# First attention: when GpSimd issues the eight row transfers of each head pair

## The reference, cut to what matters

```
scores = jnp.einsum('bhqd,bhkd->bhqk', qh, k_rec) / math.sqrt(d)
decay = jnp.exp(-LAMBDA_DECAY * jnp.abs(t[:, None] - t[None, :]))
scores = scores * decay[None, None, :, :]
attn = jax.nn.softmax(scores, axis=-1)
out = jnp.einsum('bhqk,bhkd->bhqd', attn, v_rec)
```

## Time and profile before

| what | us |
|---|---|
| median of 3 runs | 3543.53 |
| lowest, highest | 3539.63, 3559.12 |
| the profiled execution's own time | 3536.14 |
| its span, first to last instruction | 3534.2 |
| PE busy in the span | 2898.2 |
| DVE busy | 2095.9 |
| ACT busy | 1689.6 |
| POOL busy | 1095.5 |

### The profile page before, as it was taken

The page is one execution under the profiler, slowest core; times in us unless marked ns, Lnnn a source line. Parts: engine busy times, 40 slices in busy tenths (PEclk is TensorE's granted clock), DMA queues, the critical chain, the costliest instruction groups (busy, mean ns, idle before and its releaser), DMA issues. The chain is left out here.

```text
span 3534.2 us, 59852 instructions
## 1 busy us (share of the span) xinstructions
PE 2898.2 (82%) x18120; PEld 1813.4 (51%) x18120; DVE 2095.9 (59%) x4691; ACT 1689.6 (48%) x3357; POOL 1095.5 (31%) x1891
## 2 busy tenths in 40 slices
PE   6599999999983599977953999958688888797869
PEld 3234443444441589964522889824355555544434
DVE  6577777777628544445566444346477777436852
ACT  4256766677731354431122544413366667354535
POOL 3344443444401254431011544324322222020112
PEclk9679999999996799988976999979899999898879
DMA  7612222222213244330031444322211111000001
GB/s 260 228 61 74 78 73 71 76 75 76 68 60 120 73 88 90 80 76 12 0 120 54 81 93 91 58 63 83 79 50 52 50 52 51 20 1 13 0 14 48
DMA packets 171006, 248.63 MB, mean 70 GB/s; under 512 B 29752, under 2 KB 114104, under 8 KB 170832
## 3 DMA queue, kind: packets, MB, share of 16 engines
q1 hardware_dynamic: 138064, 211.81, 18.0%
q0 software_dynamic: 32768, 34.64, 6.1%
HBM read 152.94 MB, written 92.27 MB: 69 GB/s over the span
## 5 line engine op out<-in xcount | busy, mean ns | idle before, releaser
L1916 DVE CUSTOM_DVE_ANT_0 s0Ah_SD<-s0Ah_ps_s,s0Ah_table 128x1024 f32<-128x1024 f32 x512 | 607.2, 1222 | 210.7 <-PE s0Ah_ps_s L1971 164.1
L1940 ACT ACTIVATE s0Ah_PM<-s0Ah_ps_x 128x512 f32<-128x512 f32 x1024 | 533.7, 600 | 233.3 <-PE s0Ah_ps_x L1996 127.7
L1971 PE MATMUL s0Ah_ps_s<-s0Ah_plus_k,s0Ah_plus_q 48*128 48x512 f32 x1024 | 424.5, 479 | 67.4 <-DVE s0Ah_mx L1916 35.3
L1896 POOL TENSOR_TENSOR s0Ah_DG<-s0Ah_SD,s0Ah_mx 128x128 f32<-128x128 f32 x512 | 203.3, 404 | 469.4 <-DVE s0Ah_mx L1916 469.1
L1971 PEld LDWEIGHTS s0Ah_ps_s<-s0Ah_plus_k,s0Ah_plus_q 48*128 48x128 f32 x1024 | 168.1, 194 | 319.0 <-DVE s0Ah_mx L1916 214.4
L2182 ACT ACTIVATE s4Ch_PM<-s4Ch_SD,s4Ch_nb 128x260 f32<-128x260 f32 (+2 forms) x512 | 254.2, 497 | 146.0 <-POOL s4Ch_nb L2125 133.2
L2016 PE MATMUL s0Ah_ps_v<-s0Ah_PM,s0A_V 128*17 128x512 f32 x2048 | 273.6, 607 | 0.0
L2136 DVE CUSTOM_DVE_ANT_0 s4Ch_SD<-s4Ch_ps_s,s4Ch_table 128x260 f32<-128x260 f32 (+2 forms) x512 | 204.8, 407 | 77.7 <-PE s4Ch_ps_s L2227 62.1
L1996 PE MATMUL s0Ah_ps_x<-s0Ah_plus_q,s0Ah_plus_k 50*128 50x512 f32 (+3 forms) x640 | 238.3, 389 | 4.6 <-DMA s0Ah_minus_k<-s0A_parts 4.3
L2227 PE MATMUL s4Ch_ps_s<-s4Ch_ks,s4Ch_qs 96*128 96x256 bf16 (+2 forms) x896 | 141.5, 228 | 114.6 <-DVE s4Ch_mx L2136 58.8
L1996 PE MATMUL s0Ah_ps_x<-s0Ah_minus_q,s0Ah_minus_k 50*128 50x512 f32 (+3 forms) x640 | 219.0, 390 | 0.0
(11 more groups left out here) (420 smaller groups left out, 7314.4 us busy)
## 6 DMA issues: line engine op xcount, KB each, us to landing
s0A_parts<-s0Ap_sp_top SPq DMA_DIRECT2D x32, 512.0 KB, 5.4
s0A_parts<-s0Ap_sp_rest SPq DMA_DIRECT2D x32, 512.0 KB, 5.4
s1M_raw_w<-in_L_ffn_w SPq DMA_DIRECT2D x16, 1024.0 KB
s3M_raw_w<-in_L_ffn_w SPq DMA_DIRECT2D x16, 1024.0 KB
s4C_parts<-s4Cp_sp SPq DMA_DIRECT2D x48, 256.0 KB, 2.4
s0Ah_plus_q<-s0A_parts SPq DMA_DIRECT2D x64, 128.0 KB
s0Ah_plus_k<-s0A_parts SPq DMA_DIRECT2D x64, 128.0 KB
s0Ah_minus_q<-s0A_parts SPq DMA_DIRECT2D x64, 128.0 KB
```

The costliest lines, as they stand in the source:

```text
L1896: nc.gpsimd.tensor_tensor(DG[p % 3][:, r * TB + t, :], SD[i % NSD][:, t * P:(t + 1) * P], mx[p % 3][:, r * TB + t:r * TB + t + 1].to_broad ...
L1916: nc.vector.tensor_tensor_reduce(SD[i % NSD][:, :], ps_s[i % 2][:, :, :].rearrange("p a n -> p (a n)"), table[:, (TB - 1 - t) * P:(TB - 1 ...
L1940: nc.scalar.activation(PM[n % NPB][:, :], ps_x[u % NX][:, :], ACT.Exp).then_inc(e_ok, 1)
L1971: x = nc.tensor.matmul(ps_s[i % 2][:, half, :], q[at(r), t * P:(t + 1) * P], k[at(r), half * GT:(half + 1) * GT], start=True, stop=True)
```

## The change

POOL's eight transfers are no longer issued in one piece after the fourth block of the next pair. `rest_of` still stands there, but the transfers follow two at a time, behind the fifth, sixth, seventh and eighth block. For the last pair, which has no blocks behind it, all eight still follow `rest_of` directly. `maxima` takes the head and the part as arguments. The number of transfers, their order and their sizes stay as they were.

```
-            def maxima(p):
+            def maxima(p, r, n):
                 pool.wait_ge(nr_ok, START + p + 1)
-                for r in range(2):
-                    for n in range(2):
-                        for q in (plus[p % 4][0], minus[p % 2][0]):
-                            z = r * 64 + SROW + n
-                            pool.dma_start(q[z:z + 1, :].bitcast(F32).rearrange("a (t q) -> a t q", t=TB),
-                                         NMp[p % 2][n][r * TB:(r + 1) * TB, :].bitcast(F32)).then_inc(rows_in[p % 2], 16)
+                for q in (plus[p % 4][0], minus[p % 2][0]):
+                    z = r * 64 + SROW + n
+                    pool.dma_start(q[z:z + 1, :].bitcast(F32).rearrange("a (t q) -> a t q", t=TB),
+                                   NMp[p % 2][n][r * TB:(r + 1) * TB, :].bitcast(F32)).then_inc(rows_in[p % 2], 16)
...
                                         ALU.subtract).then_inc(nr_ok, 1)
-                maxima(p)
...
                 if i % U == 3 and p:
                     rest_of(p - 1)
+                if 4 <= i % U < 8 and p:
+                    maxima(p - 1, i % U // 2 - 2, i % 2)
             rest_of(NP - 1)
+            for r in range(2):
+                for n in range(2):
+                    maxima(NP - 1, r, n)
```

## The result

| | before | after |
|---|---|---|
| median us (6 runs each) | 3544.64 | 3606.68 |
| lowest, highest | 3539.49, 3566.25 | 3600.34, 3623.05 |
| span of the profiled execution | 3534.2 | 3603.4 |

The ratio is 1.0168, 95% interval 1.0136 to 1.0201. The change makes the kernel 1.7% slower, 62 us by the medians and 69 by the two profiled spans. I had forecast 17 us less, so the sign was wrong.

The account below looks back on a forecast made before the run. PE's work and the round of loads were taken as nearly equal bounds. 10.8 us from 27 pairs plus 6.0 from pair 15 made 16.8 us less, 3543.5 to 3526.7, so 3527 us; range 3512 to 3544.

Parts of the forecast that it names:

- What bounds the kernel: In the changed stage, PE's work (24.53 us a pair) and the round of loads (24.97) were said to bind almost equally.
- POOL's issuing and DVE's stall: Mid-pair, transfers issued two at a time were to remove DVE's 1.43 us wait for POOL and PE's 0.91 us.
- POOL's walk: Reckoned times of POOL's blocks and transfers after the change, the last transfer ending 17.6 us into the pair for 15.1.
- What the pair gives back: Per pair, 0.40 us less, taken from a reckoned 0.46; over 27 pairs 10.8 us.
- the reckoned 0.46: Gain per pair in us, half of PE's 0.91, with the loads' 26.30 us unchanged: 24.51 for 24.97.
- Pair 15: The pair with POOL's 3.21 us stall and the halved clock: 25.1 us expected for 31.17, a gain of 6.0.
- The 1.5 us that PE was to lose behind POOL: In pair 15, PE was to lose about this in small pieces, as POOL's stall delays later blocks.
- The other half becomes a longer wait at the pair start: The half of PE's 0.91 us not gained was to be waited out at the pair start, for the loads.
- late rows: Rival: POOL's rows land too late for PE's first `shifted`, 3554 to 3605 us; chance 0.06 together with another stall.

Follow-up runs that it names:

- e4: The kernel before, with SP loading `minus` ahead of `plus` in each round: 3526.56 us, ratio 0.9925.
- e7: The changed kernel, with each load of 32 rows split into two of 16 rows: 3485.36 us, ratio 0.9801.
- e10: The kernel before, with each load of 32 rows split into two of 16 rows: 3528.75 us, ratio 0.9939.
- e2: The changed kernel, with four unread matmuls ahead of PE's wait for the loads at each pair start: 3527.07 us, ratio 0.9913.
- e3: The changed kernel, with SP loading `minus` ahead of `plus` in each round: 3506.11 us, ratio 0.9883.
- e8: The kernel before, with four unread matmuls ahead of PE's wait for the loads at each pair start: 3553.85 us, ratio 1.0005.
- e12: The changed kernel, with two unread DVE operations (1024 and 128 columns) ahead of each eighth block: 3544.47 us, ratio 0.9972.
- e6: The changed kernel, with two unread DVE operations (1024 and 256 columns) ahead of each eighth block: 3567.71 us, ratio 1.0015.
- e1: The kernel before, with four SD buffers for DVE in place of three, POOL's transfers in one piece: 3628.3 us, ratio 1.0256.
- e9: The changed kernel, with one unread DVE operation (1024 columns) ahead of each eighth block: 3565.62 us, ratio 1.0025.
- e11: The changed kernel, with two unread matmuls ahead of PE's wait for the loads at each pair start: 3556.7 us, ratio 0.9998.

## Why the prediction was wrong

- *What bounds the kernel.* Right. PE's part of a pair and the round of loads are two legs of nearly one length; e4, e7 and e10 take one away and get the other's.
- *POOL's issuing and DVE's stall.* Right: 1.43 us of DVE and 0.91 of PE gone, POOL's walk within 0.2 us.
- *What the pair gives back.* Right in size where the clock held: 24.60 for 25.00 in six pairs, and 24.6 on average in e2. That it is 0.40 to the hundredth is luck: the 0.06 under the reckoned 0.46 was a choice, and the round took 26.54 for 26.30.
- *Pair 15.* Right that POOL's stall stays before the same transfer, that it no longer holds up PE for long and that the clock holds; the number, 25.9 for 25.1, is near by luck. The 1.5 us that PE was to lose behind POOL are one wait of 0.30, and in e7, where no load binds, pair 15 takes 24.0 for 23.6. Most of the rest is the wait for the loads at its end, 1.42 us, as in the odd pairs before it, which take 25.1 to 25.7. The stall:

```profile
641.25 0.40 POOL L1893 TENSOR_TENSOR s0Ah_DG<-s0Ah_SD,s0Ah_mx 128x128 f32<-128x128 f32 x1 [1.08 <-DVE s0Ah_mx L1918]
644.38 0.53 POOL L1883 DMA_DIRECT2D s0Ah_plus_q<-s0Ah_NM_top  x1 [2.73 <-issue]
```

- *The step that failed* is the sentence "The other half becomes a longer wait at the pair start", with no price on that wait. I had the row that warned of it: a standstill of 3.81 us had put the clock to 0.50 for 10 us. I used it for pair 15 alone, where I argued that 0.91 us had left the clock alone. I never asked what a pair start of 0.5 + 0.9 us would do, the very wait that my own sum makes. The two known sizes, 0.91 without a fall and 3.81 with one, left the whole stretch between them open, and 1.4 lies in it. What the runs showed in its place: eleven waits of 1.05 to 1.63 us at pair starts, with the clock at 0.50 behind eight of them, and nine falls in all that cost 69.8 us, four times the gain. It was a missing rival, not a mis-sized term. The row would not have told all: 13 of the 69.8 us came behind a wait of 0.64, and the kernel before had waits of 0.65 and 0.68 at pair starts without a fall.
- *The rival that came out near the number* (late rows, 3605 us) was not the cause. PE's waits at pair starts name the loads of `minus`, and POOL's queue was empty again before the pair start at 703.75. In 699 to 703 us it moved 8 packets, and in the second half of that none, since only SP's queue is left in 701 to 703:

```profile
DMA packets 30, 0.10 MB, mean 52 GB/s; under 512 B 2, under 2 KB 2, under 8 KB 30
...
q1 hardware_dynamic: 30, 0.10, 12.8%
```

The Trainium skill ("TensorE: Matmul & The Clock Gate", section on how the clock's oscillation bites in real kernels) describes a kernel in which a wait of some 3 to 5 us for a load before each tile puts the next tile's work at half clock, and advises to order the loop so that all the pieces of one output tile are done before PE waits for a load again. The runs agree that waits for loads bring the clock down, but here 0.5 to 1.7 us were enough. e3 moves and shortens the wait and e7 takes it away, and neither has a fall.

## What to carry to other kernels

Before you take a stall away from PE, follow the freed time to where it will be waited out: if a second bound lies close, short pauses merge into one longer one, and PE idles less while the clock falls. Treat TensorE's granted clock as a term of the sum for every new or longer wait, with the standstills of the trace at which it did and did not fall as bounds. The two overlap in this case, so give a fall a chance and not a threshold. Relax the second bound first (an order of loads, a shape that uses more engines); with it gone, the same change is worth its full price.

## What the runs showed of the hardware that I had not expected

- How long a standstill may be was not a matter of its length alone. In the middle of a pair, 140 waits of 0.87 to 0.94 us (the kernel before, e4, e8, e10 and e12, 28 each) were followed by no fall, and of 27 waits of 1.06 to 1.08 us in e6, 7 were. At pair starts even some of 0.48 to 0.68 us were followed by one (the changed kernel, e1, e6, e9, e11), while 12 waits up to 0.59 in e12 and 11 up to 0.68 in the kernel before were not, and three of 1.42 to 1.57 in the changed kernel were not either. What decides, the place or what PE did before, stays open; I made no run for it.
- The 40 falls between pairs 1 and 31 of the 14 traces lasted from 3.4 to 37.5 us, 26 of them over 10, though PE showed as busy in nearly all of their time. In the changed kernel a fall cost a pair 3 to 13 us, but for the one of 3.4 us.
- POOL stood 2.7 to 3.2 us before the 129th and the 249th of its 256 transfers, in all 14 traces, whatever stood between them. What it waits for stays open.
